# A graph network's first phase, split into a dense stage that stores scaled rows and an edge stage that gathers them

## The chip, the core and the metric

The kernel runs on one core of one Trainium2 chip, in float32. The metric is the device time of one launch in microseconds (us), lower is better. Times are medians of separate runs; the profile is one further execution, with its own time.

## What is computed

Four graph layers over N = 50000 nodes of 128 values, with E = 25000 edges (src, dst), sorted by dst. The change touches only the first layer and what prepares it:

```python
h = jnp.maximum(_layernorm(x, axis=-1), 0.0)
# x = x + _L0(h):
deg  = segment_sum(ones, dst with one loop per node)       # >= 1
dinv = rsqrt(deg)
norm = dinv[src] * dinv[dst]
xw   = h @ W
agg  = segment_sum(xw[src] * norm[:, None], dst) + b
x    = x + where(agg >= 0, agg, prelu_a * agg)
```

The later layers (weighted sum over edges with a product; attention with a softmax over a node's edges and a norm over all nodes; an edge network) each start from the layernormed x of the layer before and end in x plus their result.

## The kernel before

**Tiling.** Edges are cut into NT = 200 tiles of 125 edges. A tile has RW = 126 rows: row 0 is a carry row, which takes the running sum of a node whose edges began in the tile before. Tiles go in groups of GT = 4, so there are NGE = 50 edge groups. Sums over the edges of one node are products with a 0/1 selection matrix (`k_S` in the rows, `kp.S0` in the code, 126x126 for each tile), which is built from the slots' destination numbers and kept for later phases. Nodes go in wide groups of XD = 4 rows for each of 128 partitions (tiles 128x512): XG = 99 groups, two (h = 0 and 1) for each iteration.

**Phases**, one after the other, each with its own program for every engine: prep (L279, edge tables), hist (L537, degree counts by one-hot products), first (L706), second (L1157), project (L1451), softmax (L1722), attend (L1869), x3 (L2042) and mlp (L2327). A phase's block ends when all its engines do.

**Prep and hist.** Prep turns edge data into tables of slots and stores them. Meanwhile ACT's queue and SP copy x into a wider table XR (N x 130): 25 pieces of 1000 KB (`piece`, L525), 2 in prep, 12 in hist and 11 in first. Hist compares each tile's node numbers with ramps (DVE L640 and L642; ACT L680 and L682 for some tiles), multiplies the one-hot tiles on PE (L697), and ends in a table R with each node's index and dinv (`RT` on chip), stored to DRAM; first then joins it into the last two columns of XR, 25 joins of 8-byte elements. POOL gathers in prep (16), in hist (48 `hist_d`, destination rows of 12 groups, stored by SP to XD and loaded back in first; and 16 for groups 0 and 3).

**Gathers.** `gather_rows` (L530) issues one indirect DMA per tile on POOL, 126 rows each, four per group.

**First.** One loop of 50 iterations (`steps`, L75, a hardware loop over bodies of four iterations on DVE, ACT, SP and POOL; `straight`, L89, written out on PE). Iteration t does the dense rows of two wide groups and one edge group:
- dense: SP loads x; DVE takes the statistics (L883, aggregated by L898 to L908, scaled by L915 to L923); ACT makes h (L1022); PE turns it (L1085), ACT copies it out (L1001), PE multiplies by W (L1096), the PReLU is done in two parts (h = 0 on DVE, L946 and L948; h = 1 on ACT, L1010 and L1011, joined by DVE L940), PE turns it back (L1106), DVE adds x (L956), SP stores.
- edges: POOL gathers the source rows (`a_xs`, from XR; in the first NR = 16 groups from x and R apart) and the destination rows (`a_xd`); DVE takes their statistics (L889), builds the selection (L932); ACT makes messages and own rows (L1036, scaled by dinv) and copies the carry row (L993); PE sums (L1119 for the carry, L1121, L1122); ACT copies the sums (L1069), PE multiplies by W (L1152), ACT makes the parts (L1049, L1050), DVE joins them (L965), PE turns back (L1140), DVE adds the own row of x (L975), SP stores.
`ps_z`, `ps_b`, `ps_agg`, `ps_e` are one PSUM bank each; `ps_y` serves the edges and the dense h = 1 product. Each engine works in the order of its program; waits are on semaphores.

Of the kernel before, what the change touches and what calls it, by code (L numbers as in the profile page):

```python
# [26 lines left out]
N, D = 50000, 128  # L27
# [12 lines left out]
NX = (NGE - 1) // 4  # L40
# [139 lines left out]
class Keep:  # L180


    def __init__(self, m):
# [40 lines left out]
        self.s_first_idx = m.sem("first_idx")  # L224
        self.s_copied = m.sem("x_copied")
        self.s_joined = m.sem("rtable_joined")
        self.s_own = m.ring("own_gathered", NX)
# [51 lines left out]
def phase_prep(nc, m, kp, T, a):  # L279
# [3 lines left out]
    s_ix = m.ring("early_index", 4)  # L283
# [50 lines left out]
    def _(pool):  # L334
# [21 lines left out]
        for g in (1, 2):  # L356
            for w, (dst, idx) in enumerate(((kp.Xs[g], kp.irs[g]), (kp.Xd[g], kp.ird[g]))):
                pool.wait_ge(s_ix[2 * (g - 1) + w], 16 * GT)
                gather_rows(pool, dst, a["x"], idx, kp.s_gathered[g])

    @block.sync
    def _(sp):
# [31 lines left out]
        sp.wait_ge(s_rows, 128)  # L394
# [91 lines left out]
    @block.scalar  # L486
    def _(act):
        for g in (1, 2):
            for w, (idx, edge) in enumerate(((kp.irs[g], "src"), (kp.ird[g], "dst"))):
                for q in range(GT):  # L490
                    o = (g * GT + q) * EPT - 1
                    act.dma_start(idx[:, q:q + 1], a[edge][o:o + RW].rearrange("(p a) -> p a", a=1)).then_inc(s_ix[2 * (g - 1) + w], 16)
# [32 lines left out]
def piece(table, i):  # L525

    return table[i * (N // PIECES):(i + 1) * (N // PIECES), :]


def gather_rows(pool, dst, table, idx, s_rows, lo=0, hi=D):  # L530

    for q in range(GT):
        pool.indirect_dma_start(dst[:, q, lo:hi], None, table,  # L533
                                bass.IndirectOffsetOnAxis(ap=idx[:, q:q + 1], axis=0)).then_inc(s_rows, 16)


def phase_hist(nc, m, kp, T, a):  # L537
# [26 lines left out]
    RT = sb("RT", [128, NC, 2])  # L564
    psH = m.ps("count", [128, 512])
    psP = m.ps("prefix", [128, 512])
    s_set, s_d, s_one, s_pe, s_pre, s_sd, s_st = (sem("constants"), sem("dve"), sem("one_hot"), sem("counted"), sem("prefix"),
                                                  sem("root"), sem("rtable_stored"))
    s_sq, s_oneb = sem("squared"), sem("one_hot_by_scalar")
    D = [sb(f"d{j}", [RW, GT, 128]) for j in range(NX)]  # L570
    s_dg, s_ds = kp.s_own, sem("own_stored")
# [3 lines left out]
    def _(pool):  # L575
# [8 lines left out]
        for j in range(NX):  # L584
            gather_rows(pool, D[j], a["x"], kp.dsti[:, 4 * (j + 1) * GT:(4 * (j + 1) + 1) * GT], s_dg[j])
        for g in (0, 3):
            gate(kp, pool, kp.s_first_idx, max(g + 1, 3))
            gather_rows(pool, kp.Xs[g], a["x"], kp.irs[g], kp.s_gathered[g])
            gather_rows(pool, kp.Xd[g], a["x"], kp.ird[g], kp.s_gathered[g])

    @block.sync
    def _(sp):
        def keep(j):
            sp.wait_ge(s_dg[j], 16 * GT)
            sp.dma_start(slot_rows(T["XD"], j), D[j][:, :, :]).then_inc(s_ds, 16)

        for j in range(NX):
            i = EARLY + j
            sp.dma_start(piece(T["XR"], i)[:, 0:128], piece(a["x"], i)).then_inc(kp.s_copied, 16)
            keep(j)  # L600
        sp.wait_ge(s_d, 20)
        sp.dma_start(T["R"][0:MAIN, :].rearrange("(p r) c -> p r c", p=128), RT[:, 0:NF, :]).then_inc(s_st, 16)
        sp.dma_start(T["R"][MAIN:N, :], RT[0:TAIL, NF, :]).then_inc(s_st, 16)
        sp.wait_ge(s_st, 32)
        sp.wait_ge(s_ds, 16 * NX)

    @block.vector
    def _(dve):
# [6 lines left out]

        for g, ready in ((0, 3), (3, 1)):
            dve.tensor_copy(kp.irs[g][:, :], kp.srci[:, g * GT:(g + 1) * GT])
            dve.tensor_copy(kp.ird[g][:, :], kp.dsti[:, g * GT:(g + 1) * GT]).then_inc(kp.s_first_idx, ready)
# [87 lines left out]
def phase_first(nc, m, kp, T, a):  # L706
# [3 lines left out]
    X = [sb(f"x{i}", [128, XD, 128]) for i in range(8)]  # L710
    Hh = [sb(f"h{i}", [128, XD, 128]) for i in range(4)]
# [3 lines left out]
    ST = 2 * XD + 2 * GT  # L715
# [6 lines left out]
    nb = [sb(f"nb{i}", [128, 2 * XD]) for i in range(2)]  # L722

    Xs, Xd, irs, ird = kp.Xs, kp.Xd, kp.irs, kp.ird
    Xo = [sb(f"xo{i}", [RW, GT, 128]) for i in range(2)]
    dr = [sb(f"dr{i}", [RW, W4]) for i in range(2)]
    dd = [sb(f"dd{i}", [RW, GT]) for i in range(2)]
    sc = [sb(f"sc{i}", [RW, 2 * GT]) for i in range(2)]
    bi = [sb(f"bi{i}", [RW, 2 * GT]) for i in range(2)]
    M = [sb(f"m{i}", [RW, GT, 128]) for i in range(2)]  # L730
# [2005 lines left out]
```

## Time and profile before

| | before |
|---|---|
| runs | 3029.75, 3031.4, 3053.86 us; median 3031.4 |
| profiled execution | 3056.98 us, of which the span of the profile is 3055.3 us |
| granted clock, mean | 0.854 |
| busy in the span | PE 2047.6, DVE 2049.9, ACT 1734.5, POOL 1305.4 us |
| moved | 446.16 MB |
| phases, start to end | prep 0 to 42.5, hist to 199.5, first to 967, second to 1360, the rest to 3055 us |

Matmuls count on PE, weight loads (PEld) overlap them. A row of the profile's costliest groups names line, engine, operation, output and inputs, then busy us and mean ns of one instruction, then the idle time of the engine before them and what ended most of it. "issue" and "remote" as what ended it mean that the profile shows nothing that the engine waited for, and an event from outside the core's engines, in that order.

### The profile page before, as it was taken

What the parts mean: (1) busy time and instruction counts of PE and PEld (TensorE: products, weight loads), DVE (VectorE), ACT (ScalarE), POOL (GpSimd) and SP (SyncE); (2) the same over time, 40 slices, a digit from 0 to 9 for tenths busy, and PEclk for the clock granted to TensorE, in tenths of its full rate; (3) what the DMA queues carried; (4) which work ended last, traced back from release to release, by engine and by line L of the source; (5) the groups of instructions that cost most, each with busy time, mean ns of one, the idle gap of its engine ahead of it and who ended that gap; (6) DMA issues with size and microseconds to landing.
All of it is one profiled execution on the core that took longest, in us unless ns stands there. A gap on an engine that the chain in (4) does not pass through costs nothing. (4 is left out here: it accounts for less than half of the span.)

```text
span 3055.3 us, 48177 instructions
## 1 busy us (share of the span) xinstructions
PE 2047.6 (67%) x9715; PEld 1370.1 (45%) x9715; DVE 2049.9 (67%) x8012; ACT 1734.5 (57%) x4230; POOL 1305.4 (43%) x1309
## 2 busy tenths in 40 slices
PE   2235557667774455555767759966664888898997
PEld 0014445445443445545666734433332445454554
DVE  4375557777766778866656578868886665675664
ACT  1256558777775456656667724479996333333332
POOL 6525554554553655535554300000001566575574
PEclk9577779998888678777777879989998899999998
DMA  7938985544543556654444334459997533343341
GB/s 133 181 60 133 165 163 152 155 142 147 148 142 116 144 173 187 180 171 124 136 138 132 116 102 129 129 187 306 308 306 249 117 81 85 89 99 86 91 103 38
DMA packets 376243, 446.16 MB, mean 146 GB/s; under 512 B 103667, under 2 KB 225338, under 8 KB 376082
## 3 DMA queue, kind: packets, MB, share of 16 engines
q1 hardware_dynamic: 309970, 368.09, 44.1%
q0 software_dynamic: 59840, 74.08, 10.2%
q10 hardware_dynamic: 6272, 2.06, 0.4%
q8 instruction: 76, 1.25, 0.2%
q14 instruction: 85, 0.70, 0.1%
HBM read 288.86 MB, written 185.03 MB: 155 GB/s over the span
## 5 line engine op out<-in xcount | busy, mean ns | idle before, releaser
L533 POOL DMA_INDIRECT second_xs<-t_XX,second_irs x200 | 207.7, 1038 | 178.0 <-issue 70.1
L2437 POOL DMA_INDIRECT mlp_xs<-t_X,mlp_irs x200 | 203.3, 1017 | 173.3 <-issue 109.5
L2444 POOL DMA_INDIRECT out_dram<-mlp_ou,mlp_iro x200 | 216.6, 1083 | 103.6 <-issue 102.7
L2426 POOL DMA_INDIRECT mlp_bx<-t_X,k_bslot x2 | 2.0, 1016 | 597.9 <-POOLq L2710 597.6
L533 POOL DMA_INDIRECT o_xs<-t_XX,project_irs x184 | 184.0, 1000 | 168.0 <-ACT project_he L1643 99.2
L533 POOL DMA_INDIRECT a_xd<-in_x_dram,a_ird x152 | 153.0, 1007 | 232.1 <-DVE first_xo L975 195.1
L2485 DVE TENSOR_TENSOR_SCAN mlp_ms<-mlp_fm,mlp_ms,mlp_mm 128x500 f32<-128x500 f32 x98 | 121.8, 1256 | 140.9 <-ACT mlp_mm L2561 97.8
L2608 PE MATMUL mlp_ps_e<-mlp_h,mlp_we 128*128 128x504 f32 x400 | 193.0, 628 | 22.8 <-ACT mlp_h L2588 11.6
L2621 PE MATMUL mlp_ps_m<-mlp_e,mlp_wn 128*128 128x504 f32 x400 | 194.4, 610 | 0.0
L2305 PE MATMUL x_ps_o<-x_ht,x_wd 128*128 128x512 f32 (+1 forms) x198 | 117.3, 676 | 100.7 <-DVE x_ht L2202 84.1
L1119 PE MATMUL first_ps_carry<-first_m,k_S 126*126 126x128 f32 x400 | 98.2, 332 | 123.6 <-ACT first_m L993 88.5
L2561 ACT ACTIVATE mlp_mm<-mlp_ps_m,mlp_bn 128x500 f32<-128x500 f32 x100 | 66.4, 678 | 192.3 <-PE mlp_ps_m L2621 94.1
L1119 PEld LDWEIGHTS first_ps_carry<-first_m,k_S 126*126 126x126 f32 x400 | 75.0, 220 | 213.3 <-issue 213.2
L533 POOL DMA_INDIRECT a_xs<-t_XR,a_irs x136 | 137.8, 1013 | 74.5 <-issue 38.7
L1022 ACT ACTIVATE first_h<-first_x,first_nb,first_rs 128x128 f32<-128x128 f32 x391 | 159.9, 481 | 0.7 <-DVE first_nb L921 0.7
L1663 ACT ACTIVATE project_h<-project_x,project_nb,project_rm 128x128 f32<-128x128 f32 x391 | 155.3, 483 | 0.0
L2554 ACT ACTIVATE mlp_e<-mlp_ps_e,mlp_be 128x504 f32<-128x504 f32 x100 | 66.1, 677 | 147.8 <-remote 79.7
L1678 PE MATMUL project_ps_gram<-project_h 128*128 128x129 f32 (+1 forms) x782 | 132.6, 317 | 24.3 <-issue 20.9
L993 ACT ACTIVATE first_m<-first_ps_carry 1x128 f32<-1x128 f32 x199 | 50.9, 256 | 150.9 <-remote 139.9
L1678 PEld LDWEIGHTS project_ps_gram<-project_h 128*128 128x128 f32 (+1 forms) x782 | 120.8, 231 | 31.3 <-issue 24.9
L1326 ACT ACTIVATE second_hr<-second_xp,second_bi,second_rs 126x128 f32<-126x128 f32 x200 | 82.3, 482 | 83.6 <-DVE second_bi L1281 42.5
L883 DVE BATCH_NORM_STATS2 first_st<-first_x 128x6 f32<-128x128 f32 x391 | 81.7, 277 | 70.5 <-DMA first_x<-in_x_dram 49.7
(416 smaller groups left out, 6581.2 us busy)
## 6 DMA issues: line engine op xcount, KB each, us to landing
first_x<-in_x_dram SPq DMA_DIRECT2D x97, 256.0 KB
t_XX<-first_x SPq DMA_DIRECT2D x97, 256.0 KB
project_x<-t_XX SPq DMA_DIRECT2D x97, 256.0 KB
t_X<-x_x SPq DMA_DIRECT2D x97, 256.0 KB
out_dram<-x_ou SPq DMA_DIRECT2D x97, 256.0 KB
t_XR<-in_x_dram SPq DMA_DIRECT2D x23, 1000.0 KB
t_G<-second_g SPq DMA_DIRECT2D x50, 267.8 KB
t_XX<-first_xo SPq DMA_DIRECT2D x50, 252.0 KB
```

Source lines behind the costliest of these rows:

```text
L533: pool.indirect_dma_start(dst[:, q, lo:hi], None, table, bass.IndirectOffsetOnAxis(ap=idx[:, q:q + 1], axis=0)).then_inc(s_rows, 16)
L1022: ins = act.activation(Hh[2 * r + h][0:p, q, :], X[2 * u + h][0:p, q, :], ACT.Relu, bias=nb[r][0:p, c:c + 1], scale=rs[r][0:p, c:c + 1])
L1119: pe.matmul(psC[0:RW, 128 * q:128 * (q + 1)], s0, M[r][:, q, :], start=True, stop=True).then_inc(e_co, 1)
L1326: ins = act.activation(dst[:, q, :], x[:, q, :], ACT.Relu, bias=bi[k][:, w * GT + q:w * GT + q + 1], scale=rs[k][:, w * GT + q:w * GT + q ...
L1663: ins = act.activation(Hm[w][0:p, q, 0:128], X[2 * k + h][0:p, q, :], ACT.Relu, bias=nb[k][0:p, c:c + 1], scale=rm[k][0:p, c:c + 1])
L1678: ins = pe.matmul(psN[:, 0:129], Hm[w][0:p, q, 0:128], Hm[w][0:p, q, :], start=first, stop=final)
L2305: pe.matmul(featps(psO[s % 2], g), wd[:, :], feat(HTb[s % 2], g), start=True, stop=True).then_inc(s_o, 1)
L2437: pool.indirect_dma_start(Xs[u][:, q, :], None, T["X3"], bass.IndirectOffsetOnAxis(ap=irs[u][:, q:q + 1], axis=0)).then_inc(s_rows[u], 16)
L2444: pool.indirect_dma_start(out, bass.IndirectOffsetOnAxis(ap=iro[s][:, q:q + 1], axis=0), OU[s][:, q, :], None, bounds_check=N - 1, oob_is_ ...
L2485: dve.tensor_tensor_scan(Ms[r][:, h, 1:1 + E4], fm[f][:, :], Mb[r][:, h, :], init, ALU.mult, ALU.add).then_inc(s_ms, 1)
L2608: ins = pe.matmul(psE[h][:, 0:W4], we[:, w, h * 128:(h + 1) * 128], Hb[u][:, w, :], start=(w == 0), stop=(w == 1))
L2621: ins = pe.matmul(psM[h][:, 0:W4], wn1[:, w, h * 128:(h + 1) * 128], x, start=(w == 0), stop=(w == 2))
```

## The change

Prep and hist: the copy of x, the table R, the joins, the own-row table XD and all early gathers into `a_xs` go. Hist gathers the destination rows of PARKED = 18 groups (72 gathers) straight into the room of the selections, five groups ahead of where a group's selection will be written (`own`), and loads the first 8 wide groups of x; prep stores one table more, dinv by slot (`di`).

First becomes two phases:
- `phase_dense`: as the dense half of first, but h is scaled by rstd x dinv (L893 of the new kernel), POOL copies index and dinv beside it (`columns`, L773), and SP stores the 130-wide rows to a table HX. The product's two halves have own PSUM banks, as have the turned-back ones. The PReLU's join of h = 1 moves from DVE to POOL (L784, L786), between `columns` and the gathers of the other 32 groups of own rows (`park_rows`), four gathers in two of three iterations.
- `phase_edges`: POOL gathers four tiles of HX rows per group, which are the messages as they are; the carry row is written into them. The sum is multiplied by the destination's dinv on its way out of PSUM on DVE (L1039) instead of copied on ACT; the selection is one instruction of 126x504 (L1089) instead of four (before L932); the own row comes from its parked place. SP loads two broadcast rows (`dr`, `di`) for each group.

The core of the diff:

```diff
     def ahead(self, m):
...
+        self.X = [m.sb(f"x{i}", [128, XD, 128]) for i in range(8)]
+        self.Xd = [m.sb(f"xd{i}", [RW, GT, 128]) for i in range(ROOM)]
...
+    def own(self, g):
+        if known(g) and g >= NGE - ROOM:
+            return self.Xd[g - (NGE - ROOM)][:, :, :]
+        return self.rows(g + ROOM)
...
@@ phase_prep
-        for g in (1, 2):
-            for w, (dst, idx) in enumerate(((kp.Xs[g], kp.irs[g]), (kp.Xd[g], kp.ird[g]))):
-                pool.wait_ge(s_ix[2 * (g - 1) + w], 16 * GT)
-                gather_rows(pool, dst, a["x"], idx, kp.s_gathered[g])
...
-        for i in range(EARLY):
-            act.dma_start(piece(T["XR"], i)[:, 0:D], piece(a["x"], i)).then_inc(kp.s_copied, 16)
...
@@ phase_hist
+        for g in range(PARKED):
+            park_rows(pool, kp, a, g)
...
-            sp.dma_start(piece(T["XR"], i)[:, 0:128], piece(a["x"], i)).then_inc(kp.s_copied, 16)
-            keep(j)
+        for g in range(8):
+            sp.dma_start(kp.X[g][:, :, :], wide_view(a["x"], g)).then_inc(kp.s_x[g], 16)
...
@@ phase_dense, gpsimd
+        for t in range(NGE + 1):
+            if 1 < t + 1 < NGE:
+                columns(t + 1)
+            g = 2 * (t - 1) + 1
+            if there(g, XG):
+                pool.wait_ge(s_q[1], t)
+                pool.tensor_scalar(feat(Qp[1], g), feat(Qp[1], g), kp.oma[:, 0:1], None, ALU.mult).then_inc(s_qs, 1)
+                pool.wait_ge(s_qs, t)
+                pool.tensor_tensor(feat(Rp[1], g), feat(Rp[1], g), feat(Qp[1], g), ALU.add).then_inc(s_p[1], 1)
+            if parked < NGE and t % 3 < 2:
+                park_rows(pool, kp, a, parked)
+                parked += 1
...
@@ phase_dense, scalar
+        def body(t, u):
+            g1 = t - 1
+            ht(g1, 0)
+            ht(g1, 1)
...
+            parts(g1)
+            rows(t, u, 0)
+            rows(t, u, 1)
...
@@ phase_dense, tensor
+            turn(g1, u1, 0)
+            turn(g1, u1, 1)
+            back(g2, 0)
+            product(g1, 0)
+            back(g2, 1)
+            product(g1, 1)
...
@@ phase_edges, gpsimd, vector
+            if t >= 4:
+                pool.wait_ge(e_ix, t - 3)
+                pool.wait_ge(e_a, t - 3)
+            gather_rows(pool, Xs[u], T["HX"], kp.srci[:, t * GT:(t + 1) * GT], e_rows[u], XR)
...
+            stats(t, u)
+            aggregate(t, u)
+            summed(t - 3, (u - 3) % 4)
+            prelu(t - 4, u)
+            scale(t, u)
+            indices(t - 1, (u - 1) % 4)
+            final(t - 4, u)
+            select(t, u)
...
@@ phase_edges, tensor
+            sums(g2, u2, 0)
...
+                pe.matmul(psY[r3][:, 0:W4], kp.w0[:, :], AT[r3][:, :], start=True, stop=True).then_inc(e_y, 1)
+            sums(g2, u2, 1)
...
+                    ins = pe.transpose(psE[r4][0:RW, q * 128:(q + 1) * 128], Re[r4][:, q, :], kp.ident[:, :])
+                ins.then_inc(e_b, 1)
+            sums(g2, u2, 2)
+            sums(g2, u2, 3)
```

On PE, in the middle of the first phase, one iteration of the kernel before reads (`first_ps_t` is h turned, `first_ps_z` and `first_ps_y` products with W, `first_ps_b` a dense result turned back, `first_ps_e` an edge result turned back, x8 a row repeated eight times):

```order
L1085 MATMUL first_ps_t<-k_ident,first_h 128x128 x8
L1119 MATMUL first_ps_carry<-first_m,k_S 126x128
L1121 MATMUL first_ps_agg<-k_S,first_m 128x126
L1122 MATMUL first_ps_agg<-k_ident,first_hd 128x126
L1106 MATMUL first_ps_b<-k_ident,first_rp 128x128 x4
L1096 MATMUL first_ps_z<-first_ht,k_w 128x512
L1119 MATMUL first_ps_carry<-first_m,k_S 126x128
L1121 MATMUL first_ps_agg<-k_S,first_m 128x126
L1122 MATMUL first_ps_agg<-k_ident,first_hd 128x126
L1140 MATMUL first_ps_e<-k_ident,first_re 126x128 x4
```

and one iteration of the new dense stage:

```order
L922 MATMUL dense_ps_t<-k_ident,dense_h 128x128 x8
L941 MATMUL dense_ps_b<-k_ident,dense_rp 128x128 x4
L931 MATMUL dense_ps_z<-dense_ht,k_w 128x512
L941 MATMUL dense_ps_b<-k_ident,dense_rp 128x128 x4
L931 MATMUL dense_ps_z<-dense_ht,k_w 128x512
```

The edge matmuls that stood between the turns and the two products are gone to a stage of their own; the products now follow the turns with only the turned-back tiles of the iteration before between them.

On ACT one iteration before reads (`first_m` messages, `first_hd` own rows):

```order
L1060 ACTIVATE first_sd<-first_mv,k_eps 128x16
L1036 ACTIVATE first_m<-a_xs,first_bi,first_sc 126x128
L1036 ACTIVATE first_hd<-a_xd,first_bi,first_sc 126x128
L993 ACTIVATE first_m<-first_ps_carry 1x128
L1022 ACTIVATE first_h<-first_x,first_nb,first_rs 128x128 x4
L1010 ACTIVATE first_rp<-first_ps_y,k_b 128x512
L1011 ACTIVATE first_qp<-first_ps_y,k_nb 128x512
L1069 ACTIVATE first_at<-first_ps_agg 128x504
L1022 ACTIVATE first_h<-first_x,first_nb,first_rs 128x128 x4
```

and in the dense stage:

```order
L872 ACTIVATE dense_ht<-dense_ps_t 128x512 x2
L904 ACTIVATE dense_sd<-dense_mv,k_eps 128x8
L880 ACTIVATE dense_rp<-dense_ps_z,k_b 128x512
L881 ACTIVATE dense_qp<-dense_ps_z,k_nb 128x512
L893 ACTIVATE dense_h<-a_x,dense_nb,dense_rq 128x128 x8
```

The parts of the h = 1 product (L880, L881) now stand ahead of all eight rows of the next h, where before four of the eight stood ahead of them.

On POOL the dense stage has, one iteration with and one without gathers:

```order
L773 COPY dense_h<-a_RT 128x4x2 x2
L784 TENSOR_SCALAR dense_qp<-dense_qp,k_oma 128x512
L786 TENSOR_TENSOR dense_rp<-dense_rp,dense_qp 128x512
L526 DMA k_S<-in_x_dram,k_dsti 126x128 x4
L773 COPY dense_h<-a_RT 128x4x2 x2
```

POOL, which had only gathers in this phase, has two elementwise instructions for the path of the h = 1 product there, with four gathers behind them.

## Rows read from the trace of the kernel before

**Rows 1.** Busy us (instructions) by stretch; columns: us, engines, PEclk, DMA share, GB/s.

```profile
42.50:143.00 100.50, 23.72 (x75) 7.50 (x76) 33.31 (x152) 23.72 (x40) 66.29 (x70) 0.61 1.02 194
143.00:185.00 42.00, 26.53 (x127) 9.66 (x124) 41.17 (x215) 37.23 (x61) 0.00 (x0) 1.00 0.00 1
...
199.50:536.00 336.50, 197.69 (x936) 139.24 (x936) 197.74 (x808) 208.96 (x535) 186.75 (x186) 0.79 0.79 153
536.00:967.00 431.00, 304.05 (x1544) 212.22 (x1544) 310.04 (x1226) 331.96 (x854) 200.70 (x199) 0.90 0.48 143
967.00:1360.00 393.00, 205.52 (x1199) 183.35 (x1200) 292.21 (x1309) 221.62 (x553) 212.62 (x205) 0.74 0.57 167
```

**Rows 2.** Timeline of PE in prep: start, us, line, instruction, [idle before].

```profile
36.27 0.47 PE L522 MATMUL prep_ps_psC<-k_ident,prep_w 128*128 128x128 f32 x1 [10.45 <-DMA k_b<-in_L_gnn_b_dram]
```

**Rows 3.** Hist: 48 of its gathers by line; then PE's timeline after all gathers.

```profile
L533 POOL DMA_INDIRECT hist_d<-in_x_dram,k_dsti x48: 992/997/1151, 45.0 to 106.7; - x48
...
182.88 0.84 PE L697 MATMUL hist_ps_count<-hist_b,hist_a 126*128 126x391 f16 x4 [0.50 <-DVE hist_a L640]
184.23 0.84 PE L697 MATMUL hist_ps_count<-hist_b,hist_a 126*128 126x391 f16 x4 [0.50 <-DVE hist_a L640]
```

**Rows 4.** Hist, 42.5 to 143 us: waits by engine, line and releaser (us, times, longest).

```profile
DVE hist_a L640 <- issue: 35.1, 14, 7.0
...
DVE hist_a L640 <- remote: 22.1, 3, 9.0
```

**Rows 5.** Timelines of PE, ACT and DVE in the first phase: start, us, line.

```profile
679.08 1.23 PE L1085 MATMUL first_ps_t<-k_ident,first_h 128*128 128x128 f32 x8
...
681.06 0.39 PE L1121 MATMUL first_ps_agg<-k_S,first_m 126*128 126x126 f32 x2
...
681.50 0.60 PE L1106 MATMUL first_ps_b<-k_ident,first_rp 128*128 128x128 f32 x4
682.17 1.12 PE L1096 MATMUL first_ps_z<-first_ht,k_w 128*128 128x512 f32 x2
...
702.26 1.63 ACT L1022 ACTIVATE first_h<-first_x,first_nb,first_rs 128x128 f32<-128x128 f32 x4
703.80 0.66 ACT L1010 ACTIVATE first_rp<-first_ps_y,k_b 128x512 f32<-128x512 f32 x1
...
675.61 0.86 DVE L932 TENSOR_SCALAR k_S<-first_dr,k_dcol 126x126 f32 x4
...
678.69 1.64 DVE L883 BATCH_NORM_STATS2 first_st<-first_x 128x6 f32<-128x128 f32 x8
680.25 0.85 DVE L889 BATCH_NORM_STATS2 first_st<-a_xs 126x6 f32<-126x128 f32 x4
...
682.58 0.18 DVE L898 TENSOR_TENSOR first_df<-first_st 128x16 f32<-128x16 f32 x1
```

**Rows 6.** Lines of 500 to 900 us in the first phase, shapes apart.

```profile
L533 POOL DMA_INDIRECT a_xs<-t_XR,a_irs x113 | 114.5, 1013 | 61.6 <-issue 32.3 <-ACT first_m L1036 29.4
...
L533 POOL DMA_INDIRECT a_xd<-in_x_dram,a_ird x84 | 84.5, 1006 | 139.8 <-DVE first_xo L975 119.6 <-issue 20.2
...
L993 ACT ACTIVATE first_m<-first_ps_carry 1x128 f32<-1x128 f32 x113 | 28.9, 256 | 72.0 <-remote 65.8 <-PE first_ps_carry L1119 4.6 <-issue 1.6
```

**Rows 7.** One line's instructions, with first and last start; each runs once per iteration.

```profile
L975 DVE TENSOR_TENSOR first_xo<-a_xd,first_ps_e x50: 678/683/689, 241.9 to 964.5; 126x512 f32<-126x512 f32 x50
...
L1286 DVE TENSOR_TENSOR second_xp<-second_xp,second_ps_y x50: 674/686/689, 1004.2 to 1349.7; 126x512 f32<-126x512 f32 x50
```

**Rows 8.** Lines of 1010 to 1310 us, in the second phase.

```profile
L533 POOL DMA_INDIRECT second_xs<-t_XX,second_irs x166 | 172.9, 1041 | 128.1 <-issue 60.6 <-ACT second_m L1326 60.0 <-DVE second_irs L1252 7.5
...
L1286 DVE TENSOR_TENSOR second_xp<-second_xp,second_ps_y 126x512 f32<-126x512 f32 x41 | 28.1, 685 | 54.4 <-remote 51.4 <-PE second_ps_y L1398 2.4 <-issue 0.2
```

**Rows 9.** POOL's elementwise instructions, from the lines of 42.5 to 143 us.

```profile
L578 POOL MEMSET hist_zn<- 128x391 f32 x1 | 0.5, 545 | 0.0
...
L582 POOL TENSOR_SCALAR_AFFINE_SELECT hist_tri<-k_ones 128x128 f32<-128x128 f32 x1 | 0.3, 291 | 0.0
```

More of the change, by code:

```diff
@@ L393, in _ @@
             sp.dma_start(half(T["bm"], b), bm[:, b, :]).then_inc(s_rows, 16)
-        sp.wait_ge(s_rows, 128)
+        sp.wait_ge(s_f, 12)
+        for b in range(2):
+            sp.dma_start(half(T["di"], b), dinv[:, b, :]).then_inc(s_rows, 16)
+        sp.wait_ge(s_rows, 160)
         sp.wait_ge(s_gam, 48)
@@ L861, in _, with columns @@
-        steps(pool, NGE, 10, 0, body)
+        def columns(t):
+            for h in range(2):
+                g, s = 2 * t + h, (2 * t + h) % 8
+                if there(g, XG):
+                    p, n = wide_size(g)
+                    if not before(t, 4):
+                        pool.wait_ge(s_hs[s], landed(t - 4, t % 4, 4))
+                    pool.tensor_copy(Hh[s][0:p, 0:n, D:XR], kp.RT[0:p, bass.ds(wide_column(g, 0), n), :]).then_inc(s_ix, 1)
+        columns(0)
+        columns(1)
@@ L863, in _ @@
+        for s in range(4):
+            pool.wait_ge(kp.s_own[s], 16 * GT * len(range(s, NGE, 4)))
     @block.vector
     def _(dve):
-        def indices(g, s):
-            if there(g, NGE) and not before(g, 4):
-                dve.wait_ge(s_rows[s], complete(g - 4, s) + gathered[s])
-                dve.tensor_copy(irs[s][:, :], kp.srci[:, bass.ds(g * GT, GT)])
-                dve.tensor_copy(ird[s][:, :], kp.dsti[:, bass.ds(g * GT, GT)]).then_inc(e_idx, 1)
         for i in range(2):
@@ new lines, in select, with final @@
+        def select(t, u):
+            if there(t, NGE):
+                r = u % 2
+                dve.wait_ge(e_dr[r], landed(t, r, 2))
+                if not before(t, ROOM):
+                    dve.wait_ge(e_x1, t - ROOM + 1)
+                dve.tensor_tensor(kp.selections(t), dr[r][:, :].rearrange("p (q e) -> p q e", q=GT),
+                                  kp.dcol[:, bass.ds(t * GT, GT)].unsqueeze(2).to_broadcast([RW, GT, RW]), ALU.is_equal).then_inc(e_s0, 1)
+        def final(g, u):
+            if there(g, NGE):
+                r = u % 2
+                dve.wait_ge(e_b, g + 1)
+                if not before(g, 2):
+                    dve.wait_ge(e_s1[r], landed(g - 2, r, 2))
+                dve.tensor_tensor(Xo[r][:, :, :], kp.own(g), psE[r][0:RW, :].rearrange("p (q d) -> p q d", q=GT), ALU.add).then_inc(e_x1, 1)
@@ new lines, in _, with sums @@
+    @block.tensor
+    def _(pe):
+        def sums(g, u, q):
+            if not there(g, NGE):
+                return
+            r = u % 2
+            if q == 0:
+                pe.wait_ge(e_s0, g + 1)
+                if not before(g, 2):
+                    pe.wait_ge(e_at, g - 1)
+            pe.wait_ge(e_hd, g * GT + q + 1)
+            gate(kp, pe, e_ci, g * GT + q + 1)
+            s0 = kp.select(g, q)
+            pe.matmul(psC[0:RW, 128 * q:128 * (q + 1)], s0, Xs[u][:, q, 0:D], start=True, stop=True).then_inc(e_co, 1)
+            ag = psA[r][:, q * RW:(q + 1) * RW]
+            pe.matmul(ag, Xs[u][:, q, 0:D], s0, start=True, stop=False)
```

556 lines of the change are left out of this document (258 added, 298 removed).

## Prediction

> **What bounds the kernel now.** I read the kernel by stretches first, then the timelines inside the stretches that the change touches, then the waits. The stretches [rows 1] show that the change works on everything up to 967 us: prep and hist, 199.5 us, and the first phase, 767.5 us. From 967 us on the program is the same.
>
> Prep ends late because PE's last turn (L522) waits 10.45 us for a load of a weight [rows 2], while sixteen gathers and the first copies of x are in the DMA queues.
>
> In hist DVE sets the pace. Once no gather is left, four tiles take 1.35 us (from 182.88 to 184.23 us [rows 3]) and DVE is busy 41.17 of 42 us [rows 1]. While gathers run, DVE is busy 33.31 of 100.5 us, and its L640 stood idle 35.1 us with nothing to wait for and 22.1 us for something outside the core [rows 4]: 57 us. POOL's gathers come every (106.7 - 45.0) / 47 = 1.31 us [rows 3].
>
> The first phase runs at (964.5 - 241.9) / 49 = 14.75 us per iteration [rows 7]: 336.5 us for the first 20, where copies and joins fill the DMA engines (share 0.79), 431 us for the other 30 (0.48) [rows 1]. ACT is busiest (331.96 of 431 us) and works through its rows without a gap, apart from standstills: the copy of the carry row (L993) sat idle 65.8 us for something outside, in 400 us with 113 + 84 = 197 gathers [rows 6]. I price that as 65.8 / 197 = 0.33 us per gather. The second phase, which has four gathers per iteration and no dense part, gives nearly the same: 51.4 us of "remote" before L1286, 166 gathers, 0.31 us each [rows 8]. It runs at (1349.7 - 1004.2) / 49 = 7.05 us per iteration [rows 7].
>
> **Prep and hist: about 47 us less.** Without the gathers, the index loads and the copies, L522 need not wait: prep ends up to 10.45 us earlier, near 32 us. Added are two stores of dinv, beside eight others, a microsecond at most. Then hist on DVE: some 4.6 us of setting up, 50 groups x 1.35 us = 67.5 us, and a tail of 10.5 us give 115 us if nothing disturbs it. POOL issues 72 gathers, 72 x 1.31 = 94 us, to about 128 us, under DVE's work. At 0.33 us per gather they cost DVE 24 us: 139 us. Held as much as before, hist would end near 195 us. I take 152 us, nearer to the first, since the 14 copies of 1000 KB and the 12 stores, which were part of a DMA share of 1.02 [rows 1], are gone, and the price of 0.33 was seen at a share near 0.5. That saves 199.5 - 152 = 47 us; the ends are 4 and 60 us. The eight loads of x lie under hist, and spare the dense stage its first wait.
>
> **The dense stage: about 472 us.** Its bound is no engine's work but a loop through PE and ACT, which the order of both shows. The edge matmuls and edge rows, which stood between, are gone, and with them the work that filled the waits. From the last row of h: turn of h = 1 (half of 1.23 us, 0.6), turn back 0.6, product 1.1, turn back 0.6, product 1.1, together 4.0 us on PE; then the two parts on ACT, which now stand ahead of all rows (two like L1010's 0.66, overlapped, 1.2); then eight rows of h, 2 x 1.55 = 3.1 us [rows 5]. That is 8.3 us. ACT's own work is less (3.1 + 1.2 + two copies like L1010 1.2 + the root 0.3: 5.8 us), DVE's too (8 statistics 1.64, five small 0.9, two additions of x 1.4, the scaling 0.6, the PReLU of h = 0 1.5: 6.0 us). POOL: the two elementwise instructions are not in the trace of before with these operands. Below, 512/391 of 0.545 us, 0.7 each; above, four times 0.29 us, 1.2 each [rows 9]; I take the upper. With the column copies (0.4) and four gathers (5.2) POOL has at most 8.0 us per iteration, and the result is wanted only 3.1 + 0.6 + 0.6 + 1.1 = 5.4 us after the parts: this move costs nothing. Should POOL take over 5.4 us for the two, the excess is paid 50 times. The stores of HX (99 of some 266 KB) go through SP, with two loads and two stores beside them per iteration: loads of x and stores of the new x 25.6 MB each, HX 26 MB and gathers 8 MB are 85 MB, in 460 us 185 GB/s; 42.5 to 143 us moved 194, so I count no wait for it [rows 1].
>
> With 128 gathers over 50 iterations, 2.56 each, standstills add 2.56 x 0.33 = 0.85: 9.15 us per iteration, 457 us, with 15 us for filling 472 us. The ends are 430 us without standstills and 520 us if the clock falls too (below).
>
> **The edge stage: about 390 us.** The bound is a loop through DVE: the sums out of PSUM (0.68, as L975 [rows 7]), the product on PE 1.1, the sums of another tile 0.75 (three like the 0.39 of L1121, overlapped), the turn back 0.6, the final addition 0.68, the selection (one instruction of the size of L975, 0.68, where the four took 0.86), four statistics 0.85, five small ones 0.9 [rows 5]: 6.2 us. POOL needs 4 x 1.31 = 5.2 us, hidden. With four gathers, 1.3 us of standstills: 7.5 us. The second phase, with the same gathers and more work on DVE, runs at 7.05 [rows 7]. I take the middle, 7.3: 365 us and 25 us for filling five groups deep make 390. The ends are 6.2 x 50 + 25 = 335 and 7.8 x 50 + 25 = 415 us.
>
> **The sum.** First phase 767.5 us before, 472 + 390 = 862 us after: +94. The reason: without standstills one iteration took 12.0 us before (431 / 30 = 14.4, less 2.4 of standstills, for 197 x 14.4 / 400 = 7.1 gathers at 0.33), in which the dense loop and the edge loop overlapped; apart, each runs at its own latency, 8.3 + 6.2 = 14.5 us, +2.5 us 50 times, +125 us. Against that the first 20 iterations lose the 2.4 us that they took longer than the rest (336.5 / 20 = 16.8), -48 us, standstills fall by 0.4 us per iteration, -20 us, and two fillings add 40 us: again about +95. The removed work (200 message rows on ACT, 200 statistics on DVE) shortens engines that bound neither stage. With -47 us ahead: +47 us. The profiled execution (3057 us) would become 3104 us, the median of the runs, 26 us lower, 3031.4 + 47 = 3079 us.
>
> **Rivals.**
> *The standstills go with the loops' length (faster).* The programs' loop bodies shrink by half: of four iterations DVE's from 229 rows to 106 and 119, ACT's from 157 to 81 and 85. If what stalls the engines is fetching the next part of a loop and not the gather, the standstills go: 8.3 x 50 + 15 + 6.2 x 50 + 25 = 765 us, no more than before, and the 47 us ahead remain: 2984 us. It turns to the faster side where the standstills of both stages, 42 + 55 = 97 us by my sum, fall below half. The Trainium skill ("Runtime: NRT & Kernel Launch", Instruction fetch mechanics) says that an engine holds only two pages of instructions and that a jump to a target outside them forces a fetch before it can go on; by that the short bodies would stall less. Against it: the second phase's bodies (139 rows on DVE, 63 on ACT) are as short, and still lose 51.4 us of 300 [rows 8]; and hist ran at full pace once the gathers had ended [rows 3].
> *Hist is held as before (slower).* If the gathers alone caused the 57 us of [rows 4], 72 of them hold hist until their last data land, near 136 us, with 42 groups still to do; the dense stage starts at about 195 us and only 4 us are saved: 3031 + 94 - 4 = 3121 us. For it: the pace came back with the end of the gathers, not of the copies.
> *PE's clock falls in the dense stage (slower).* In the second phase PE is busy 52% and the granted clock is 0.74; in the second part of the first, 71% and 0.90 [rows 1]. In the dense stage PE would be busy 4.4 of 9.15 us. At 0.74 half of the time is at the low level instead of a fifth, which makes the 4.0 us of PE in the loop 1.5/1.2 as long, +1.0 us, 50 times: 3079 + 50 = 3129 us. The Trainium skill ("TensorE: Matmul & The Clock Gate", Part 1) says that the clock follows how busy PE has been of late; the two stretches agree in direction.
>
> **How the numbers follow.** My forecast 0.48 (its own range 3030 to 3115 us), the first rival 0.22, held hist 0.17, the clock 0.13. The range must reach into the first rival (2984) and past the last (3129): 2985 to 3140. About 1% (30 us) is what a measurement can tell from no change: below 3001 us faster, above 3062 slower. The first rival gives faster 0.20 and same 0.02; my forecast same 0.17 and slower 0.31; the other two slower 0.30. So faster 0.20, same 0.19, slower 0.61.
>
> **What would show it.** The dense stage's start near 152 us (195: held hist; under 130: no standstills). The dense iteration, by the start of L904 on ACT: 9.15 us on average, with parts (L880) waiting for PE each time; 8.3 or less means the first rival, above 10 the clock, which the stretch's granted clock tells. "Remote" idle near 40 us in dense and 60 in edges. The edge iteration by L1098: 7.3 us. If PE's turn back of h = 1 (L941) waits for POOL's L786, my price of POOL is wrong. Wrong altogether would be the forecast if ACT's rows do not wait behind the parts for PE, since the loop of 8.3 us is the term on which the sum rests.

## The result, and the profile after

The changed kernel takes 3146.1 us (median of four runs, 3138 to 3152), the one before 3030.6: the ratio is 1.039 with an interval of 1.034 to 1.044. It is slower by 3.9%; forecast was 1.6%, 3079 us in 2985 to 3140. Beside each other on another chip the ratio was 1.033 (1.028 to 1.038), below.

The profiled execution of the changed kernel took 3149.4 us in its span, 94.1 us more than the one before (3055.3). The medians stand 115 us apart, since the profiled execution before was 26 us above its median, and this one 5 us.

| stretch, us | before | after | forecast |
|---|---|---|---|
| prep and hist | 199.6 | 192.8 | 152 |
| first / dense | 768.7 | 505.8 | 472 |
| edges | in the 768.7 | 357.2 | 390 |
| the rest | 2087.0 | 2093.6 | as before |

The stretches of after show it (columns: us, then busy us with instructions for PE, PEld, DVE, ACT and POOL, then the granted clock, the DMA share and GB/s):

```profile
32.00:128.00 96.00, 20.51 (x60) 6.20 (x60) 25.27 (x113) 18.34 (x30) 73.47 (x75) 0.58 0.23 69
128.00:192.80 64.80, 32.45 (x144) 11.91 (x144) 56.92 (x262) 43.11 (x71) 0.02 (x1) 0.84 0.00 1
192.80:700.00 507.20, 335.46 (x980) 205.97 (x980) 314.53 (x1000) 274.81 (x638) 283.29 (x326) 0.67 0.50 165
700.00:1051.00 351.00, 255.00 (x1496) 204.67 (x1496) 225.84 (x842) 197.76 (x550) 215.15 (x200) 0.90 0.59 146
```

From 32 to 128 us, while POOL gathers, DVE is busy 25.3 of 96 us, with the DMA engines used 23% only and not 102% as in [rows 1]. In the dense stage the granted clock is 0.67, against 0.79 and 0.90 in the first phase before [rows 1]. One line of ACT, once per iteration, gives the pace, (688.5 - 195.6) / 49 = 10.06 us, and from the sixth on 10.2 us, settling at 10.24:

```profile
L904 ACT ACTIVATE dense_sd<-dense_mv,k_eps x50: 291/292/306, 195.6 to 688.5; 128x8 f32<-128x8 f32 x50
```

The timelines of PE and ACT of one dense iteration:

```profile
399.92 1.11 PE L922 MATMUL dense_ps_t<-k_ident,dense_h 128*128 128x128 f32 x4 [2.90 <-ACT dense_h L893]
401.47 1.11 PE L922 MATMUL dense_ps_t<-k_ident,dense_h 128*128 128x128 f32 x4 [0.43 <-ACT dense_h L893]
402.37 1.06 PE L941 MATMUL dense_ps_b<-k_ident,dense_rp 128*128 128x128 f32 x4
403.23 1.92 PE L931 MATMUL dense_ps_z<-dense_ht,k_w 128*128 128x512 f32 x2
404.93 1.06 PE L941 MATMUL dense_ps_b<-k_ident,dense_rp 128*128 128x128 f32 x4
405.79 1.48 PE L931 MATMUL dense_ps_z<-dense_ht,k_w 128*128 128x512 f32 x2
...
407.31 0.69 ACT L880 ACTIVATE dense_rp<-dense_ps_z,k_b 128x512 f32<-128x512 f32 x1 [3.90 <-PE dense_ps_z L931]
407.89 0.68 ACT L881 ACTIVATE dense_qp<-dense_ps_z,k_nb 128x512 f32<-128x512 f32 x1
408.46 3.19 ACT L893 ACTIVATE dense_h<-a_x,dense_nb,dense_rq 128x128 f32<-128x128 f32 x8
```

From the turn of h = 1 (401.47) to the parts (407.31) PE takes 5.84 us; L880 stood idle 3.90 us for it. Parts and rows follow, and PE waits 2.9 us for the first four of them (the row at 399.92). The same matmuls took about half as long in [rows 5]: 0.60 us for four turned-back tiles there, 1.06 here; 1.12 for a product, 1.92 and 1.48 here. Cut into two stretches, the iteration shows why (columns as above):

```profile
400.00:406.60 6.60, 6.17 (x19) 4.15 (x20) 2.96 (x8) 2.68 (x7) 1.53 (x3) 0.50 0.45 160
406.80:410.00 3.20, 0.47 (x2) 0.00 (x0) 3.02 (x11) 2.69 (x6) 1.33 (x1) 1.00 0.51 164
```

While PE works, the granted clock is 0.50 (the low level, 1.2 GHz); while PE stands idle for ACT's rows, it is 1.00 (2.4 GHz), and it has fallen again when the next turns start. So the mean of 0.67 says too little: nearly all of PE's work is done at the low level. The waits of the stage, by line:

```profile
ACT dense_rp L880 <- PE dense_ps_z L931: 183.1, 48, 3.9
...
PE dense_ps_t L922 <- ACT dense_h L893: 174.9, 98, 14.1
DVE a_x L849 <- PE dense_ps_b L941: 148.0, 91, 3.5
...
PEld dense_ps_b L941 <- POOL dense_rp L786: 0.2, 1, 0.2
```

PE and ACT wait for each other, 175 and 183 us; PE's weight load for POOL 0.2 us. There is no row of "remote" in that window. And hist's waits:

```profile
ACT hist_sq L658 <- remote: 70.5, 9, 9.8
...
DVE hist_a L618 <- remote: 60.6, 9, 9.8
...
PE hist_ps_count L675 <- remote: 31.4, 5, 9.0
```

### The profile page after: what moved, and what is told of

It is laid out like the page before. It is cut to its first block and busy times, and to the rows that moved or that the text cites. A ratio compares the mean times of both kernels' runs of the same rounds, so it can differ in the third digit from the quotient of the medians.

```text
span 3149.4 us, 48533 instructions
## 1 busy us (share of the span) xinstructions
PE 2155.8 (68%) x9715; PEld 1441.7 (46%) x9715; DVE 2081.0 (66%) x7817; ACT 1670.3 (53%) x4030; POOL 1407.0 (45%) x1442
## 5 line engine op out<-in xcount | busy, mean ns | idle before, releaser
L526 POOL DMA_INDIRECT edges_xs<-t_HX,k_srci x200 | 215.9, 1079 | 121.7 <-PE edges_ps_agg L1184 54.3
L922 PE MATMUL dense_ps_t<-k_ident,dense_h 128*128 128x128 f32 x391 | 108.9, 434 | 174.9 <-ACT dense_h L893 174.9
L2663 PE MATMUL mlp_ps_e<-mlp_h,mlp_we 128*128 128x504 f32 x400 | 202.5, 654 | 33.1 <-issue 14.2
L526 POOL DMA_INDIRECT k_S<-in_x_dram,k_dsti x180 | 182.0, 1011 | 51.5 <-issue 51.5
L922 PEld LDWEIGHTS dense_ps_t<-k_ident,dense_h 128*128 128x128 f32 x391 | 69.9, 216 | 248.5 <-ACT dense_h L893 248.4
L849 DVE TENSOR_TENSOR a_x<-a_x,dense_ps_b 128x512 f32<-128x512 f32 (+1 forms) x99 | 67.5, 682 | 163.6 <-PE dense_ps_b L941 148.0
L1733 PE MATMUL project_ps_gram<-project_h 128*128 128x129 f32 (+1 forms) x782 | 140.3, 321 | 47.4 <-issue 44.7
L931 PE MATMUL dense_ps_z<-dense_ht,k_w 128*128 128x512 f32 (+1 forms) x198 | 163.9, 929 | 0.0
L893 ACT ACTIVATE dense_h<-a_x,dense_nb,dense_rq 128x128 f32<-128x128 f32 x391 | 156.1, 491 | 0.7 <-DVE dense_nb L832 0.7
L784 POOL TENSOR_SCALAR dense_qp<-dense_qp,k_oma 128x512 f32<-128x512 f32 (+1 forms) x49 | 76.2, 1555 | 179.2 <-ACT dense_qp L881 179.2
```

What stands on the lines that cost most here:

```text
L526: pool.indirect_dma_start(dst[:, q, 0:hi], None, table, bass.IndirectOffsetOnAxis(ap=idx[:, q:q + 1], axis=0)).then_inc(s_rows, 16)
L893: ins = act.activation(Hh[2 * u + h][0:p, q, 0:D], X[2 * u + h][0:p, q, :], ACT.Relu, bias=nb[r][0:p, c:c + 1], scale=rq[r][0:p, c:c + 1])
L922: ins = pe.transpose(o[:, q, :], Hh[2 * u + h][0:p, q, 0:D], kp.ident[0:p, 0:p])
L931: pe.matmul(featps(psZ[h], g), kp.w0[:, :], feat(HTr[h], g), start=True, stop=True).then_inc(s_z, 1)
L1733: ins = pe.matmul(psN[:, 0:129], Hm[w][0:p, q, 0:128], Hm[w][0:p, q, :], start=first, stop=final)
L2663: ins = pe.matmul(psE[h][:, 0:W4], we[:, w, h * 128:(h + 1) * 128], Hb[u][:, w, :], start=(w == 0), stop=(w == 1))
```

## The experiments

Each kernel is the changed one with an edit. They ran in four sets, each set on a chip of its own with the kernel before beside it. That one took 3021 us on the chips of the first two sets, 2584 us on the third, and 3073 us on the fourth; ratios are taken within a set. Where only one run is given, no interval can be.

**Parts behind rows** (parts_last), in the dense stage's ACT program:

```diff
-            parts(g1)
             rows(t, u, 0)
             rows(t, u, 1)
+            parts(g1)
```

> The changed kernel with one edit in the dense stage: on ACT the two parts of the h = 1 product stand behind the eight rows of the next h instead of ahead of them. Theory 1 (the loop turn, product, parts, rows sets the pace; it runs at 10.24 us per iteration since the low clock stretches its PE part): the loop is cut, the iteration falls to what the busiest engine or queue asks, 6 to 7.5 us, the dense stage from 507 to about 350 us, the run to about 3146 - 150 = 2995 us. Theory 2 (the memory traffic of the dense stage, 165 GB/s, or POOL sets the pace): no change, 10 us per iteration. Theory 3 (only the clock matters): the iteration stays above 8.3 us.

Measured: 3038.7 us, 1.008 of before (1.004 to 1.012). The dense iteration is 7.95 us, the clock 0.88. The loop is cut, and what is left is a wait that had been hidden:

```profile
PE dense_ps_b L941 <- POOL dense_rp L786: 88.4, 46, 3.8
...
ACT dense_rp L880 <- PE dense_ps_z L931: 6.3, 8, 1.1
...
L904 ACT ACTIVATE dense_sd<-dense_mv,k_eps x50: 292/301/302, 195.8 to 585.5; 128x8 f32<-128x8 f32 x50
```

From 200 to 580 us L880 waits 6.3 us for PE, where in the changed kernel it waited 183.1 us over the whole stage, and PE's turn back now waits 88 us for POOL's join, which stands behind POOL's gathers. So theory 1 holds in kind, and theory 2 is out: 208 GB/s and POOL's work fit into 7.95 us. This one edit of the order gave 2.1 us per iteration, but the clock rose with it, from 0.67 to 0.88, and the run can't part the two. Nor does it put theory 3 out: at the high clock the loop that was not cut takes 7.68 us (fill, below), also less than 8.3. That the order gives something of its own is shown by the later kernels with 7.28 and 6.95 us, less than 7.68.

**Idle matmuls** (fill), behind the last product of each iteration, into a bank of their own:

```diff
             product(g1, 1)
+            if there(g1, NGE):
+                for i in range(16):
+                    pe.matmul(psF[:, 0:128], kp.w0[:, :], kp.ident[:, :], start=True, stop=True)
```

> The changed kernel with 16 matmuls of 128x128 added behind the last product of each dense iteration, into a bank of PSUM that nobody reads, where PE now stands idle for 2.9 us. Theory 1 (the loop with PE at the low clock): the granted clock of the stage rises from 0.67 towards 1, and though PE does more, the iteration falls from 10.24 to 8.3 to 8.8 us, the run to about 3146 - 80 = 3066 us. Theory 2 (traffic or POOL sets the pace): no change in the iteration. Theory 3 (the clock does not follow PE's idle time): clock 0.67 and the iteration grows by the added work, to over 12 us.

Measured: 3017.8 us, 0.999 of before (0.996 to 1.002).

```profile
192.70:577.00 384.30, 358.60 (x2564) 297.67 (x2565) 286.85 (x991) 274.10 (x638) 281.15 (x325) 0.99 0.66 218
...
399.51 0.66 PE L923 MATMUL dense_ps_t<-k_ident,dense_h 128*128 128x128 f32 x4 [0.42 <-ACT dense_h L894]
...
401.74 1.02 PE L932 MATMUL dense_ps_z<-dense_ht,k_w 128*128 128x512 f32 x2
402.60 3.73 PE L956 MATMUL dense_ps_fill<-k_ident,k_w 128*128 128x128 f32 x32
...
402.80 0.69 ACT L881 ACTIVATE dense_rp<-dense_ps_z,k_b 128x512 f32<-128x512 f32 x1 [1.81 <-PE dense_ps_z L932]
...
403.95 3.18 ACT L894 ACTIVATE dense_h<-a_x,dense_nb,dense_rq 128x128 f32<-128x128 f32 x8
```

With 16 matmuls more (32 rows of the trace) each iteration takes 7.68 us instead of 10.24, at a granted clock of 0.99. From the turn of h = 1 to the parts PE now takes 402.80 - 399.51 = 3.29 us, 2.55 us less than 5.84: that is the whole difference between 10.24 and 7.68, and the rest of the loop, on ACT, is 4.4 us in both. Nothing of the kernel's own work was changed, so the clock is the cause of it. It is below my 8.3 to 8.8 us too, since the loop at the high clock is 7.7 us and not 8.3.

**No gathers in hist** (no_hist):

```diff
-PARKED = 18
+PARKED = 0
...
-            if parked < NGE and t % 3 < 2:
+            if parked < NGE:
```

> The changed kernel with no gather in hist: all 200 gathers of own rows in the dense stage, four in each iteration. Theory A (gathers in close sequence hold up hist's other engines): hist ends at 31 + 4.6 + 50 x 1.35 + 10.5 = 114 us and not 193, so up to 79 us go; the dense stage keeps its 10.24 us, since POOL has 0.4 + 2.9 + 5.2 = 8.5 us of work in it. The run: about 3070 us. Theory B (something else than the gathers slows hist, such as the first loads of x): hist still ends near 190 us, the run stays at 3146. If the gathers cost the dense stage 0.33 us each, as I forecast, 72 more of them give 24 us back.

Measured: 3056.1 us, 1.014 of before (1.008 to 1.021). Hist's last work ends at 113.2 us and the dense stage starts at 113.8, 79 us earlier; theory A holds, and the eight loads of x, which are still there, are not the cause.

```profile
31.00:113.80 82.80, 44.17 (x204) 16.41 (x204) 80.27 (x378) 61.46 (x101) 1.92 (x6) 0.96 0.08 25
113.80:617.00 503.20, 333.98 (x980) 204.34 (x980) 313.15 (x992) 274.06 (x638) 354.01 (x395) 0.67 0.54 175
...
31.00:192.80 161.80, 52.96 (x204) 18.12 (x204) 83.11 (x378) 61.45 (x101) 74.49 (x78) 0.69 0.14 42
```

DVE is busy 80.3 of 82.8 us, against 83.1 of 161.8 in the changed kernel with its gathers (the last row). The dense iteration stays at 10.24 us with four gathers in each and no row of "remote": in a loop of this length they cost nothing.

**How the gathers stand in hist** (hist8, hist8_spaced). Both park 8 groups in hist and 42 in dense; hist8_spaced waits between:

```diff
         for g in range(PARKED):
+            if g:
+                pool.wait_ge(s_pe, 6 * g)
             park_rows(pool, kp, a, g)
```

> The changed kernel with 8 groups (32 gathers) parked in hist, back to back, and the other 42 in dense, one in each of 42 iterations. If the hold comes only from gathers behind a dozen or so others, hist ends at 114 us plus some 20 us, near 135 us; if each gather costs the same 79 / 72 = 1.1 us, at 149 us.

> As hist8, but each four gathers in hist wait until PE has counted six more groups of tiles (about 8 us), so never more than four follow each other. If the sequence without pauses is what holds the other engines, hist ends at 114 to 118 us. If the number of gathers is, it ends as in hist8.

```profile
31.00:143.50 112.50, 49.05 (x204) 17.42 (x204) 82.59 (x379) 61.47 (x101) 34.54 (x39) 0.82 0.12 37
...
31.00:114.90 83.90, 44.74 (x204) 16.78 (x204) 80.94 (x379) 61.50 (x101) 36.02 (x39) 0.94 0.16 50
```

The same 32 gathers back to back hold hist until 143.5 us, 29.7 us more than none; four at a time with pauses until 114.9, 1.1 us more. (As single runs 3094 and 3052 us.) So neither the number of gathers nor their traffic holds the others, but gathers that follow each other without a pause; and of the 32, each cost 0.93 us, of the 72 each 1.10. These are two single runs, but the ends of hist lie 28.6 us apart. What in the chip holds the engines is open. It is not the loading of instructions: in the changed kernel's hist, ACT's L658 was held before each of nine iterations in a row, not once per loop body of four, and from 32 to 128 us the trace has one packet of instructions among the DMA packets (queue, packets, MB, share):

```profile
q0 software_dynamic: 3414, 4.59, 16.4%
q1 hardware_dynamic: 1129, 2.05, 6.2%
q14 instruction: 1, 0.01, 0.0%
```

**The join of h = 1 on DVE** (prelu_dve), with POOL's two instructions taken out:

```diff
+            g = 2 * t + 1
+            if there(g, XG):
+                dve.wait_ge(s_q[1], t + 1)
+                dve.scalar_tensor_tensor(feat(Rp[1], g), feat(Qp[1], g), kp.oma[:, 0:1], feat(Rp[1], g), ALU.mult, ALU.add).then_inc(s_p[1], 1)
```

> The changed kernel with the PReLU's join of h = 1 back on DVE, as in the kernel before; POOL only copies columns and gathers in the dense stage. By the prediction's step (POOL's work is hidden) nothing changes: 10.24 us per iteration. The rival, that PE's turn back waits for POOL's 1.57 + 1.27 us, gives up to 2 us less per iteration, 3050 us.

Measured: 3165 us in one run, and the same pace:

```profile
L905 ACT ACTIVATE dense_sd<-dense_mv,k_eps x50: 291/292/301, 195.9 to 689.4; 128x8 f32<-128x8 f32 x50
```

That is (689.4 - 195.9) / 49 = 10.07 us. The move to POOL cost the dense stage's pace nothing in the changed kernel.

**Both, in two ways** (pl_dve, pl_nohist_dve, pl_dve2).

> The changed kernel with the parts behind the rows (as in parts_last) and the PReLU's join of h = 1 on DVE (as in prelu_dve). In parts_last the wait that was left was PE's turn back L941 for POOL's L786, 88 us, since POOL's gathers stood ahead of it. Theory: each edit's cost shows only where the other's is gone; here the iteration falls from 7.95 to 6.8 to 7.2 us (DVE's work), where prelu_dve alone gave nothing. Rival: memory traffic (215 GB/s in parts_last) holds it at 7.9.

> As pl_dve, and no gather in hist (four in each dense iteration). The gains should add: hist ends at 114 us as in no_hist, the dense iteration takes about 7 us (POOL has 5.6 us of work), so 3146 - 80 - 50 x 3.1 = about 2915 us, below the kernel before. Rival: 72 more gathers and 40 GB/s more traffic slow the dense stage, 7.5 to 8 us per iteration and 2950 us.

Measured: 3150.6 us (one run), and with no gathers in hist 3099.4 us, 1.023 of before (1.016 to 1.029). My theory missed a loop:

```profile
DVE dense_rp L835 <- ACT dense_qp L882: 169.7, 45, 4.4
ACT dense_sd L905 <- DVE dense_mv L819: 166.0, 44, 4.0
```

DVE stands still 170 us for the parts, which ACT makes after the rows; the statistics behind that wait hold ACT's next root and rows, 166 us. The iteration is 10.3 us again on average (10.4 with no gathers in hist), and the granted clock of the stage 0.71, so here too the low clock has a share that was not measured. In pl_dve2 the join stands one iteration later:

```diff
                 aggregate(t, u)
+            join(t - 2)
             dense_x(g2, u2, 0)
```

> As pl_dve, but DVE joins the h = 1 parts one iteration later in its order, between the statistics and the additions of x, so that it need not stand still for the parts that ACT now makes last. In pl_dve DVE waited 170 us for them and ACT 166 us for DVE in turn: a loop rows, parts, join, statistics, scale. Theory: with that loop cut too, DVE's work is what is left, 6.8 to 7.4 us per iteration, about 3146 - 150 = 2995 us. Rival: traffic holds the stage at 7.6 us or more whatever the order.

Measured: 6.95 us per iteration, as the theory says. It ran on the third chip, 2613 us in one run, where the kernel before took 2584.

**The third chip** (pl_dve2_spaced, fill_spaced_dve, backs_first ran there too).

> As pl_dve2, with hist as in hist8_spaced (8 groups parked in hist, four gathers at a time with pauses). The two causes should add: hist ends at 115 us (78 less), the dense stage at 7 us per iteration (150 less): 3146 - 228 = about 2920 us, 3.5% below the kernel before. Rival: the dense stage pays for the 42 groups of gathers that it takes, 2950 us.

> The other way to the same end: the parts stay ahead of the rows, 16 idle matmuls per iteration keep PE busy as in fill, the join of h = 1 is on DVE and hist is as in hist8_spaced. The loop at the high clock took 7.68 us in fill; with hist at 115 us the run should take 3018 - 78 = about 2940 us. If POOL or traffic had a part in the 7.68 us it falls or rises from there.

Measured: 2605.4 us, 1.008 of before (1.006 to 1.010), and 2649.4 us, 1.025 (1.023 to 1.027), with 6.86 and 7.64 us per dense iteration. The forecasts, made for chips of the first kind, fell: the kernel before gains 440 us on this chip (no trace of it was taken there). None of the four traces of this set, backs_first included, has a row of "remote", and pl_dve2, with all 72 gathers back to back in hist, ends hist at 114 us:

```profile
31.00:114.00 83.00, 44.66 (x204) 16.48 (x204) 80.76 (x378) 61.59 (x101) 64.50 (x66) 0.95 0.24 71
```

So the hold by gathers and the standstills of the other phases were absent on this chip and present on the three others. It was tried once; what differs in it is not known.

**Turned-back tiles first** (backs_first):

```diff
+            back(g2, 0)
+            back(g2, 1)
             turn(g1, u1, 0)
             turn(g1, u1, 1)
-            back(g2, 0)
             product(g1, 0)
-            back(g2, 1)
             product(g1, 1)
```

> The changed kernel with PE's order in the dense stage changed alone: both turned-back tiles ahead of the turns, where PE waits for ACT's rows, instead of between turns and products. Theory (the loop is turn, backs, products, parts, rows): the loop loses the two backs, 2 x 0.86 us at the low clock: 8.5 us per iteration if the clock stays at 0.67, less if it rises, about 3060 us. If the iteration stays at 10.24 us, it is not that loop that sets it.

Measured: 2766 us (one run), 10.27 us per iteration: the expectation failed. The timeline of PE names a new wait:

```profile
403.63 1.12 PE L941 MATMUL dense_ps_b<-k_ident,dense_rp 128*128 128x128 f32 x4 [2.96 <-POOL dense_rp L786]
404.54 1.92 PE L922 MATMUL dense_ps_t<-k_ident,dense_h 128*128 128x128 f32 x8
406.45 3.09 PE L931 MATMUL dense_ps_z<-dense_ht,k_w 128*128 128x512 f32 x4
```

The turn back of h = 1 waits 2.96 us for POOL's L786, now ahead of the turns, and PE runs at the low clock (0.68 over the stage): parts, POOL's 2.8 us, turn back, turns and products are a new loop. The edit doesn't tell whether the first loop lost its two turns back. Its iterations settle at 10.2 to 10.3 us, the length of the changed kernel's, though its terms are others; why two loops at the low clock settle at one length is open, and a sum of durations doesn't explain it.

**Before and after on one chip** (before_again, after_again, pl_dve2_spaced_b, fill_b).

> The kernel before, unchanged, for a trace of it on the chip of this call: the last call's chip ran it in 2584 us, those of the two calls before in 3021 us. Theory: the difference lies in the standstills, so on a chip of the first kind hist ends near 130 us and the first phase near 12 us per iteration, with next to no waits for something outside; on one of the second kind the rows are as first read.

> The changed kernel, unchanged, beside the one before on the same chip. On a chip without standstills: hist ends at 114 us, but the dense iteration is 10.24 us as everywhere, since the loop with the low clock owes nothing to them; before has 12 us or less per iteration there. So the change costs more there than 3.9%: 2766 / 2584, some 7%. On a chip with them 3.9% as before.

> The kernel with parts last, the join later on DVE and spaced gathers in hist. On the last chip it was 0.8% slower than before. On a chip with standstills it should be faster than before by 2 to 3.5% (3146 - 78 - 150 = 2920 us of 3021); on one without, 0.8% slower again.

> The changed kernel with the 16 idle matmuls, again: 7.68 us per dense iteration on every chip. Beside after_again on the same chip it should save 50 x 2.5 = 120 us.

This chip was of the first kind: before_again 3077 us, hist held until 199.2 us, the first phase 768.6 us. after_again 3173.9 us, 1.033 (1.028 to 1.038), 10.24 us per dense iteration. fill_b 3050.2 us, 0.991 (0.988 to 0.994), 7.68 us: 124 us less than after_again, as expected. pl_dve2_spaced_b 2977.1 us, 0.969 (0.965 to 0.973), 3.1% faster than the kernel before:

```profile
31.00:114.70 83.70, 44.70 (x204) 16.69 (x204) 80.75 (x378) 61.48 (x101) 35.83 (x38) 0.94 0.16 50
114.70:481.00 366.30, 227.82 (x980) 125.79 (x980) 298.29 (x1041) 270.38 (x638) 195.29 (x267) 0.91 0.70 235
483.00:846.00 363.00, 255.68 (x1500) 204.41 (x1500) 227.76 (x850) 197.02 (x550) 211.21 (x200) 0.89 0.56 142
```

Hist ends 80 us earlier than in after_again and the dense stage takes 366 us, 7.28 us per iteration. Both causes are taken out here together; on this chip they were not tried one by one, except the clock in fill_b. What the unedited change costs on the third chip was not measured.

## Why the prediction was wrong

**What bounds the dense stage: right in kind.** The loop through PE and ACT was named, and L880 waits for PE in each iteration. Its size was not: at the high clock it takes 7.68 us (fill), not 8.3, since PE's part overlaps more (3.29 us, not 4.0).

**The clock: one of two steps that failed.** The main case took the loop's PE part, 4.0 us, at the durations of [rows 5], and left the low clock to a rival with 0.13. The part took 5.84 us: the low clock cost 2.56 us per iteration, by that sum 128 us over the stage (fill_b saves 124 us of the run), where the rival's sum had 50. The clock was 0.67, lower than the 0.74 of that rival, but its way of pricing failed too. It spread the mean clock evenly over PE's work (by 1.5/1.2; the ratio of the means, 0.90 to 0.74, is 1.22). Spread evenly, 0.99 against 0.67 would make 3.29 us into 4.9; it was 5.84, since the low stretch covers PE's work and the high one its pause. The working itself held what tells it: a loop in which PE waits for ACT's rows leaves PE idle once per iteration, and the matmuls of [rows 5] were measured where edge matmuls stood between. That their removal let the clock fall is argued from this; shown is that added matmuls bring it back.

**Standstills in the dense stage: wrong.** The 0.33 us per gather of [rows 6] was forecast as 0.85 us per iteration. There were none, with 2.56 gathers per iteration (changed kernel) or with 4 (no_hist). In the shorter loop of pl_dve2_spaced_b, three rows of "remote" add up to 15.8 us, and pl_dve2_spaced, the same kernel, takes 0.4 us less per iteration on the third chip; so they were not gone for good, and still cost little. In the changed kernel the 0.85 us and the loop's 0.6 us too much make 1.47 us too much, against 2.56 too little for the clock, which makes 10.24 of 9.15: the stage took 506 us, not 472.

**Hist: the other step that failed.** It saved 6.8 us, not 47. Prep's part was right: hist begins 12 us earlier (30.7 against 42.8 us). But the gathers held it as before, at a DMA share of 0.23: the rival "held hist". What failed is the price: 0.33 us per gather from a phase where at most eight follow each other, used for 72 in a row, which cost 1.10 each. The reason I gave for staying near it, that the copies were gone, was no cause. The right row was [rows 4], 57 us in the same place; hist8 against hist8_spaced shows the cause, gathers without pauses.

**The edge stage: right in kind, too high.** 6.52 us per iteration (L1098), not 7.3, and 357 us, not 390. Without standstills, on the third chip, the same instruction comes every 5.95 us (pl_dve2_spaced), near the 6.2 of the sum. The standstills cost 0.6 us and not 1.1 (0.7 between pl_dve2_spaced and pl_dve2_spaced_b, the same kernel on both chips). Per gather that is 0.14 to 0.19 us, about half of the price.

**POOL's work: right that it is hidden.** prelu_dve doesn't change the pace. The two instructions took 1.57 and 1.27 us, more than the 1.2 each that were the upper price, and well under the 5.4 us that they had. But they were hidden only while the loop was long: in parts_last POOL's join is the wait.

**The rival of faster** (standstills go with the loops' length) named something that happened in the dense stage of the changed kernel, where they did go. Its time of 2984 us failed for the clock and hist. That the loops' length is the reason is not shown: hist's loops are short, and its standstills depend on the pauses between gathers. The Trainium skill's rule on instruction pages ("Runtime: NRT & Kernel Launch", Instruction fetch mechanics) says that a jump out of the pages held costs a fetch; the trace of hist does not show it, with one packet of instructions beside nine held iterations, and hist8 and hist8_spaced have the same loops on DVE. For the standstills of the other phases it was not tested.

**The sum.** Against the forecast of +47 us, hist gave +41, the dense stage +34, the edge stage -33, the rest of the program +7: +96, and the profile has +94. That the two new stages together (863 us) came out at my 862 is a chance of two errors. The rivals were weighed as if only one of them could come true. Held hist (+43 us, 47 less 4) and the low clock (+50) came together: added to the forecast of 3079 us by their own sums they give 3172, beyond the range of 2985 to 3140, and the edge stage (33 us cheaper) and the missing standstills of the dense stage brought it back to 3146.

## What to carry to other kernels

When a change takes matmuls out of a loop, ask what kept PE's clock up there, and price the loop's PE part wholly at the low clock, not at the mean: a loop in which PE waits once per turn can settle at it, and 16 matmuls that compute nothing were worth 124 us here. An order in which an engine makes the waiting result first (parts ahead of rows) closes such a loop; moving it behind independent work opened it, and each opened loop showed the next (POOL, then DVE), so measure the cuts together. Put gathers in fours with pauses beside other work, not in a row. And ask of two rivals whether both can come true, before the range is set.

## What the hardware showed that I had not expected

- Gathers back to back (1.3 us apart) delay the other engines: with 72 in a row DVE, ACT and PE waited up to 9.8 us at a time for something outside the core, and hist took 79 us longer; the 32 with pauses cost 1.1 us. On one of the four chips there was no such thing, and the kernel before ran 15% faster; the reason is open.
- The dense loop settled at 10.24 us to within 0.02 us for some 40 iterations, in the changed kernel, after_again, no_hist and hist8, with the granted clock at 0.67: 0.50 while PE worked and 1.00 while it waited. With the added matmuls it settled at 7.68 us and 0.99. The Trainium skill ("TensorE: Matmul & The Clock Gate", Part 1) says that the clock follows how busy PE has been; the trace agrees, 0.99 with the pause filled against 0.67.
